# Banded attention in a decoder kernel: products of query and key in pairs of half-heads, four pairs of a chunk made by GpSimd

## The reference

```python
deltas = [0, 1, ..., 40, 128, 96, 384]      # distances to a key, J = 44
q, k, v = split(x @ w_qkv)                  # 16 heads of 16 features
idx   = arange(T)[:, None] - deltas         # T = 112 tokens
valid = idx >= 0
scores = einsum('bhtd,bhtjd->bhtj', q, k[idx] * (1 + scale_embed)) / sqrt(16)
scores = where(valid, scores + pos_bias.T, -max)
out   = einsum('bhtj,bhtjd->bhtd', softmax(scores), v[idx]) * if_gain
return out @ w_out
```

## Time and profile before

| what | value |
|---|---|
| median of 3 runs | 3439.84 us (3436.94 to 3442.88) |
| profiled execution | 3413.12 us, its span (first to last instruction) 3411.2 us |
| span's share of PE, DVE, ACT, POOL | 90%, 53%, 35%, 29% |
| banded attention | about 21 us (first product) to 325.8 us of the span |
| TensorE's granted clock in its four chunks | 1.00 of full speed |

### The profile page before, as it was taken

One profiled execution on the slowest core, in us unless ns is written; L12 is line 12 of the kernel. 1 busy time (PEld: TensorE's weight loads), 2 busy tenths in 40 slices (PEclk: granted clock), 3 DMA queues, 4 the chain that ended last, 5 costly groups with the idle time before them and its releaser, 6 DMA issues. The chain is left out here.

```text
span 3411.2 us, 72275 instructions
## 1 busy us (share of the span) xinstructions
PE 3068.7 (90%) x29076; PEld 2124.1 (62%) x29076; DVE 1814.2 (53%) x4513; ACT 1181.2 (35%) x2319; POOL 995.6 (29%) x822
## 2 busy tenths in 40 slices
PE   8997999999988888889678999699997999889989
PEld 3434555555667865658345555489997886666656
DVE  7897544453334655433776666543333763455543
ACT  1223333332233431313326665222222652244433
POOL 1001443343102111426248878321111211104001
PEclk9998999999998999989889999799998999999989
DMA  4223000000222022527211110378886200121100
GB/s 156 65 75 100 10 9 18 9 9 0 54 58 26 7 52 74 150 79 255 70 33 31 32 31 19 110 292 329 328 328 230 77 2 13 37 73 51 49 14 19
DMA packets 174741, 287.70 MB, mean 84 GB/s; under 512 B 79393, under 2 KB 145025, under 8 KB 165102
## 3 DMA queue, kind: packets, MB, share of 16 engines
q1 hardware_dynamic: 166958, 263.07, 24.0%
q0 software_dynamic: 7488, 20.46, 1.8%
HBM read 245.07 MB, written 28.48 MB: 80 GB/s over the span
## 5 line engine op out<-in xcount | busy, mean ns | idle before, releaser
L2852 PE MATMUL ps<-L_ffn_xsT,arena 128*128 128x128 f32 x2584 | 304.0, 276 | 0.7 <-DVE L_ffn_xsT L2651 0.6
L2852 PEld LDWEIGHTS ps<-L_ffn_xsT,arena 128*128 128x128 f32 x2584 | 296.3, 193 | 3.6 <-DVE L_ffn_xsT L2651 3.5
L842 POOL TENSOR_TENSOR L_xattn_rn<-L_xattn_ss,mhalf 125x16 f32<-125x16 f32 (+1 forms) x64 | 185.8, 2903 | 257.3 <-DVE L_xattn_ss L905 257.3
L3534 POOL TENSOR_TENSOR L_xattn_pT<-L_xattn_pT,L_xattn_keep 125x678 int32<-125x678 int32 x128 | 190.4, 1509 | 62.6 <-ACT L_xattn_pT L3789 62.6
L162 POOL TENSOR_TENSOR rstd<-nsc,mhalf 112x4 f32<-112x4 f32 (+2 forms) x26 | 40.2, 1545 | 556.0 <-DVE nsc L155 555.0
L2750 ACT ACTIVATE L_ffn_silu<-ps,arena 128x128 f32<-128x128 f32 x280 | 102.9, 368 | 269.2 <-PE ps L2852 254.0
L2660 DVE SCALAR_TENSOR_TENSOR L_ffn_hT<-ps,arena,L_ffn_silu 128x128 f32<-128x128 f32 x280 | 98.0, 350 | 155.3 <-ACT L_ffn_silu L2750 155.1
L2529 POOL DMA_INDIRECT L_ffn_rows_out<-L_ffn_ys,L_ffn_dest x78 | 79.6, 1021 | 319.8 <-DVE L_ffn_ys L2669 304.1
L1019 PE MATMUL ps<-arena,L_xattn_cT 128*125 128x512 f32 x384 | 166.1, 592 | 0.0
L723 PE MATMUL ps<-L_attn_prod,arena 128*32 128x448 f32 (+28 forms) x672 | 153.5, 492 | 11.5 <-DVE L_attn_prod L523 10.9
L2865 PE MATMUL ps<-arena,L_ffn_hT 128*128 128x256 f32 x646 | 153.0, 381 | 5.5 <-ACT L_ffn_ys L2759 5.4
(11 more groups left out here) (616 smaller groups left out, 6753.2 us busy)
## 6 DMA issues: line engine op xcount, KB each, us to landing
arena<-in_L_ffn_up SPq DMA_DIRECT2D x35, 2056.0 KB, 8.1
arena<-in_L_ffn_down SPq DMA_DIRECT2D x35, 1152.0 KB, 8.6
L_xattn_ctxT<-in_ctxT SPq DMA_DIRECT2D x48, 375.0 KB, 3.7
arena<-in_L_ffn_up SPq DMA_DIRECT2D x43, 384.0 KB, 4.5
L_attn_a<-L_attn_skew SPq DMA_DIRECT2D x16, 784.0 KB, 5.2
L_xattn_ctx<-in_ctx SPq DMA_DIRECT2D x30, 375.0 KB
arena<-L_xattn_kp SPq DMA_DIRECT2D x64, 93.8 KB, 3.3
L_xattn_mask<-in_mask SPq DMA_DIRECT2D x32, 164.1 KB, 8.4
```

What stands on the lines that cost most here:

```text
L842: nc.gpsimd.tensor_tensor(rn[0:r, i], ss[0:r, i], core.mhalf[0:r, 0:H], ALU.pow).then_inc(po_r.step("root", i), 1)
L2852: ins = nc.tensor.matmul(ps[:, 2 + b % 4, half * TS:(half + 1) * TS], self.up(i % WU, k, half * HM + m), xsT[:, i % 2, k], start=(k == 0), ...
L3534: nc.gpsimd.tensor_tensor(p, p, keep[:, n % 2].unsqueeze(1).to_broadcast([SP_, 2, ST * TP]), ALU.mult).then_inc(po_e.step("kept", half), 1)
```

## The change

- **Pairs.** One instruction makes the products of both halves of a distance: 42 instructions of twice the size in place of 84. `turn_of` is changed with it: in a block of 16, matmuls i and i+2 are now the two halves of one distance and go to the same column group; four matmuls in a row are groups 0, 1, 0, 1, then 2, 3, 2, 3. A pair fills slots `i % 8` and `(i + 2) % 8`; its instruction waits for both slots to be free (`before`). The ring no longer shifts by chunk: the first pair of a chunk waits for matmul 82 of the chunk before.
- **Fewer masked tokens.** Where the accumulator already holds finite numbers (everywhere but in the first two blocks of chunk 0), the even distance of a group is computed only for the tokens that its group needs. In those two blocks of chunk 0, both halves are computed for all tokens.
- **Subtraction in memory order.** `below` walks `e` as it is stored, with the maximum repeated over the distances.
- **GpSimd.** Pairs 15, 23, 31 and 39 of each chunk are made by GpSimd, which waits for the same slots and counts on a semaphore of its own (`po_i`).

The diff, cut to its core:

```diff
-        ve_x, ve_i, ve_g = one("vector", "xn", U), one("vector", "prod", NI), one("vector", "biased", NG)
+        ve_x, ve_i, ve_g = one("vector", "xn", U), one("vector", "prod", NI // 2 - SHARE), one("vector", "biased", NG)
+        po_i = one("gpsimd", "prod", SHARE)
...
             at, groups = i % 16, -(-size(i // 16) // 32)
-            c, b, odd = at % groups, at // groups % KD, at // groups // KD
+            apart = groups // 2 or 1
+            c, b, odd = at // (apart * KD) * apart % groups + at % apart, at // apart % KD, at // groups // KD
...
-            return 0 if odd == 0 and b == 0 else self.DIST[p]
+        def first_of(n):
+
+            apart = -(-size(n // 8) // 32) // 2 or 1
+            return n // 8 * 16 + n % 8 // apart * KD * apart + n % apart, apart
+
+        def start(c, i):
+
+            p, _, _, odd = turn_of(i)
+            if odd:
+                return self.DIST[p]
+            return 0 if c == 0 and i < 32 else min(self.DIST[p:p + 2])
+
+        def made(c, n):
+
+            if n % 8 == 7:
+                return (po_i, c, n // 8 - 1) if n > 8 else (ve_i, c, n)
+            return (ve_i, c, n - max(n // 8 - 1, 0))
+
+        def before(i):
+
+            return i - RING if i >= RING else max(n for n in range(NI) if n % RING == i) - NI
+
+        def products(eng, own, c, n):
+            i, apart = first_of(n)
+            if n == 0 or own is nc.gpsimd:
+                eng.wait_ge(ac_q.sem, ac_q.at(c, "qk", 2 * KD - 1))
+            used = max(before(i), before(i + apart))
+            if used >= 0:
+                eng.wait_ge(pe_i.sem, pe_i.at(c, "used", used))
+            elif c:
+                eng.wait_ge(pe_i.sem, pe_i.at(c - 1, "used", NI + used))
+            j, t0, at = self.DIST[turn_of(i)[0]], start(c, i), i % RING
+            by, _, m = made(c, n)
+            own.tensor_tensor(prod[:, at:at + apart + 1:apart, :, t0:T], q[:, c % 2].rearrange("p b (u t) -> p b u t", u=U)[:, :, :, t0:T],
+                              k[c % 2][:, :, :, PAD + t0 - j:PAD + T - j], ALU.mult).then_inc(by.step("prod", m), 1)
...
             norm_pool(core, norm)
+            products(pool, nc.gpsimd, 0, 15)
             nc.gpsimd.memset(k[1], 0.0).then_inc(ready, 1)
             nc.gpsimd.memset(v[1], 0.0).then_inc(ready, 1)
+            for c in range(NCH):
+                for n in range(15 if c else 23, NI // 2, 8):
+                    products(pool, nc.gpsimd, c, n)
...
-                nc.vector.tensor_tensor(by_head(e[c % 2][:, u]), by_head(e[c % 2][:, u]), mx[:, u, :].unsqueeze(2).to_broadcast([T, H, J]),
+                row = e[c % 2][:, u].rearrange("p (j h) -> p j h", h=H)
+                nc.vector.tensor_tensor(row, row, mx[:, u, :].unsqueeze(1).to_broadcast([T, J, H]),
...
-                    product(c, i)
+                    if i % 2 == 0:
+                        if made(c, i // 2)[0] is ve_i:
+                            products(dve, nc.vector, c, i // 2)
...
-                ten.wait_ge(ve_i.sem, ve_i.at(c, "prod", i))
+                by, _, m = made(c, pair_of(i))
+                ten.wait_ge(by.sem, by.at(c, "prod", m))
```

25 lines of the change are left out of this document (7 added, 18 removed).

## The result

The changed kernel takes 3445.56 us (median of 20 runs, 3439.83 to 3453.0) beside 3440.37 us for the kernel before (20 runs on the same chip): ratio 1.0015, 95% interval 1.0009 to 1.0021. It is 5 us slower where 10 us faster was forecast. The time is inside the range (3415 to 3450), the sign is wrong.

The account below looks back on a forecast made before the run. VectorE and TensorE were taken to run in lockstep, TensorE's pace limiting the middle chunks. Chunks +1.0, -2.6, -3.0, -5.2 and ending -0.4 made -10.2 us: 3439.8 to 3429.6, range 3415 to 3450.

Parts of the forecast that it names:

- Products, VectorE's time: VectorE's products, paired and with fewer masked tokens: -4.7 us in each of chunks 1 to 3, -2.6 in chunk 0.
- Subtraction: VectorE's subtraction in memory order, 1.21 to 0.77 us: -0.44 each, four in each of chunks 1 to 3, -1.8.
- The ending's -0.4: In the ending only the first subtraction counts, -0.4 us; the others sit behind the transfers.
- GpSimd's share: VectorE rid of 3.6 us per chunk but blocked 4.0 (chunk 0: 5.5) by GpSimd's products: net +0.4, chunk 0 +1.9.
- TensorE's own work: TensorE's matmuls in chunks 1 to 3: fewer tokens -1.7 us, runs of one column group +1.0, net -0.7 per chunk.
- What TensorE lets through: Share of VectorE's gain that shortens chunks: half of TensorE's waits in chunks 1 and 2 (-3.0, -3.4), -5.0 in chunk 3.
- New waits: First pair of a chunk waits for matmul 82: +1.2, +0.6, +0.6 us at the boundaries; shrunken lead +0.5 per chunk.
- the lead shrinks from 8 products to 5 or 6 ... taken +0.5: Pairs need two free slots, so VectorE's lead over TensorE shrinks: bounds 0 and +2 us per chunk, taken +0.5.
- the first (eaten up, 3440): Rival: TensorE bounds chunks 1 and 2 and GpSimd blocks fully, together +0.6 us; 3440, between 3434 and 3446; chance 0.25.
- The second: Rival: GpSimd is free, streaming products don't block VectorE's, -3.6 us per chunk for the share; together -27, 3413; chance 0.12.
- The third, the slower one: Rival: GpSimd can't get the port from dense VectorE products, +2.0 us at ten places; +8 in all, 3448; chance 0.18.

Follow-up runs that it names:

- sub_alone: Kernel before with only the subtraction in memory order; the two middle chunks fell by 0.93 and 1.00 us, the last by 1.4.
- no_share: Changed kernel with all 42 pairs on VectorE, none on GpSimd; 72.38 us per middle chunk, 52.6 us in chunk 0, as slow as the changed kernel.
- ring_on: Changed kernel with the ring of slots running on over the end of a chunk; the stop at a chunk's start was worth 0.8, 0.9 and 0.9 us.
- ring12_no_share: Changed kernel with twelve slots, all 42 pairs on VectorE and the context loaded by ScalarE's queue; 69.57 us per middle chunk.
- singles_masks: Kernel before with only the subtraction in memory order and the changed kernel's masks; 12 us faster than before (0.35%, interval 0.24 to 0.47%).
- ring12_share123: Changed kernel with twelve slots, GpSimd's share in chunks 1 to 3 only, context loaded one block earlier than in ring12_no_share; ratio 0.9977 to the kernel before.
- ring12: Changed kernel with twelve slots, context loaded by SyncE after the last matmul; chunks together 11.9 us shorter than the changed kernel's, ending lost 6.6.
- fills_first: Changed kernel with GpSimd's clearing of k[1] and v[1] put ahead of its first pair; chunk 0 1.1 us shorter, chunk 3 1.5 us longer.
- singles_c0_busy: singles_masks_c0 with 15 more matmuls in the ending, results read by nobody; the ending takes 40.6 us.
- singles_masks_c0: singles_masks with the masks of the kernel before in the first two blocks of chunk 0; chunk 0 fell by 1.10 us to 48.88.

## Why the prediction was wrong

From before to after there is a ladder of rungs (column "last"): subtraction, 262.73 to 259.53, -3.2 us; masks, to 253.66, -5.9; order, to 256.04, +2.4; pairs in eight slots, with the stop at the chunk's start, to 265.50, +9.5 (1.9, 2.9, 2.9 and 1.8 by chunk); share, to 264.78, -0.7. The good half of the change was worth 9 us, the other half cost 11.

- *Products, VectorE's time.* Right: pairs of 840 to 872 elements take 1.03 to 1.07 us as records (by the formula 0.94 to 0.98, and the overlap), and VectorE's busy time in chunk 1 fell by 8.4.
- *Subtraction.* Right: 0.86 us, and half let through. The ending's -0.4 did not come (sub_alone: +0.1).
- *GpSimd's share.* The step put +0.4 us on VectorE per chunk and +1.9 in chunk 0. That a product waits for GpSimd's is right, but it was counted too often. In chunk 1 no_share's 59.93 us less 3.6 would be 56.3 and 57.23 was measured, so 0.9 was blocked, not 4.0; one VectorE product is stretched there, at 142.06, from 1.09 to 1.75 us. In chunk 0 four are, by 3.0 us in all, not 5.5. The net in time is -1.14 in the middle chunks and +1.35 in chunk 0: the sizes were off by 0.5 to 1.5 us and the sign in the middle. In chunk 0 most of the cost came by a way not named: the fills beside L198.
- *TensorE's own work.* -0.7 as a net was mis-sized: the masks gave 2.25, 2.22, 2.02 us (with VectorE's shorter products in it) and the order took 0.56, 0.55, 0.60, -1.4 to -1.7 in all. The reading of the order was loose, too: in the four runs named a group comes back after one other (3, 2, 3, 0), not directly. Chunk 0, for which I had counted the wider first blocks on VectorE alone, lost 0.6 by the masks and 0.7 by the order.
- *What TensorE lets through.* Half of VectorE's gain, -5.0 in chunk 3: true of the subtraction (0.93, 1.00 and 1.4 of 1.8), untrue of the pairs. Pairs took 3 us per chunk off VectorE and gave, even in twelve slots, +0.1 in the middle chunks and -0.3 in chunk 3 (66.05 against 66.35). This step failed as well, in chunk 3 above all. It stood on a sum of waits and not on what each edit does to the moment at which a product is there.
- *New waits.* **This is the step that failed most.** At the chunk's start 1.2, 0.6, 0.6 were forecast, 0.8, 0.9, 0.9 measured (ring_on): right in sum. But "the lead shrinks from 8 products to 5 or 6 ... taken +0.5" was 2 us per chunk: no_share less ring12_no_share, 2.8, less the 0.85 of the start; in chunk 0, 4.55 less 0.8. Its upper bound of 2 was the truth in chunks 1 to 3, and chunk 0 went beyond it. The reason for the low value, that the full lead had been used up in only 14 places for 12.4 us, is a reading of a queue with eight units of one, and says nothing of one with four units of two. The place to look at was the dense run of matmuls that ends with matmul 75: the loss turned up right behind it.

The forecast by chunk was +1.0, -2.6, -3.0, -5.2 and -0.4 for the ending; measured +4.65, -0.88, -0.89, -0.83 and +1.0. Of the 13.3 us between the sums, the lead explains some 7.8: 3.75 us of chunk 0 and 2 of each other chunk, less the 0.5 counted. In chunk 3 another 2.9 are missing, which the pairs did not let through. The ending's 1.4 are not explained by any edit here: it varies from 40.1 to 42.6 us among the kernels that load the context as before does.

Of the rivals, the first (eaten up, 3440) has the nearest time but not the reason: GpSimd didn't block fully, and the middle chunks came down to 68.9 us (singles_masks), so TensorE did not bound them at 72. The second fell (products beside GpSimd's take 1.5 to 2.2 us, so streams do block). The third, the slower one, forecast 3448 by GpSimd not getting in. Its mechanism exists, in three places of sixteen: VectorE products that started behind GpSimd's pair ran ahead of it, once each at 110.8 and 182.0 us, and three of them here (GpSimd, then VectorE):

```profile
235.96 3.85 POOL L409 TENSOR_TENSOR L_attn_prod<-arena 128x696 f32<-128x696 f32 x1 [21.80 <-PE ps L756]
```

```profile
235.38 0.86 DVE L526 TENSOR_TENSOR arena<-arena,L_attn_mx 112x672 f32<-112x672 f32 x1
236.16 2.36 DVE L409 TENSOR_TENSOR L_attn_prod<-arena 128x648 f32<-128x648 f32 x3
238.44 1.32 DVE L532 TENSOR_REDUCE L_attn_den<-arena 112x16 f32<-112x672 f32 x1
```

GpSimd's pair, 1.51 us beside a reduction (at 99.19), started during the subtraction and was done only 1.4 us after the reduction began; three products that started after it went through first. But as no_share is as slow as after, the rival's account of the loss is wrong.

Left open: the changed kernel's 5.2 us are 1.9 more than the stage of its profiled execution shows. A half-clock stretch in chunk 3 (three of the four kernels with after's schedule there had one at this place) and a longer ending would be enough, but no profile of such an execution of after exists. Why chunk 3 takes 66.4 us in ring12_share123 and 65.2 in ring12 wasn't followed (0.8 of it arises between matmuls 24 and 28, and ring12 is the one with a half-clock stretch ahead of them), nor why pairs with the old masks and twelve slots stay 0.8 us above single products (72.32 against 71.20 and 0.3 for the order) where with the new masks they are level.

## What to carry over

Count a ring of buffers in the producer's units: eight slots filled two at a time are a lead of four at most, and of fewer where the two of a pair come free at different moments, and an engine that got faster by pairing will wait for it. The price falls due where the consumer takes unit after unit without other work. Split a bundle of edits and take each to the engine that bounds: here shorter matmuls and a faster subtraction were worth 10 to 12 us by themselves (stage, whole), and the larger part, fewer and longer VectorE instructions, was worth nothing with twelve slots and cost 9.5 with eight. Where two engines run in lockstep, one that is busy for 65.6 of 72.5 us may still give its saved time back as waiting.

## What the runs showed of the hardware

- A stop of 1.93 us of TensorE, with work up to it and behind it, went with some 3 us at 1.2 GHz in three kernels and not in a fourth with the same stop (after); those three took 1.5 us more. What a half-clock stretch costs depends on where it falls: the one at matmul 20 of chunk 3 (no_share, fills_first) was made up by matmul 24. In chunk 0 singles_c0_busy had the clock at 0.5 from 22.0 to 25.4 us and took 48.89 us, singles_masks_c0, with the same code there and the clock at 1.00, 48.88: where products set the pace, the half clock cost nothing. The Trainium skill (TensorE: Matmul & The Clock Gate, What's actually happening) says that idleness throttles the array and that activity releases it. The three kernels agree, and the fourth, whose clock stayed at 1.00 there, shows that the same stop does not always do it.
- GpSimd's memory fills, which read nothing, held VectorE's tensor-scalar instructions (one input in SBUF): 3.27 us for four in place of 1.37. The Trainium skill (SBUF — State Buffer, Who interferes with whom) counts tensor_scalar among the instructions that can take the port pair that VectorE and GpSimd share; the rows agree.
- The same section says that whoever issues first gets the port pair. In the place above (235.96 us) three VectorE products that started 0.2 to 1.7 us after GpSimd's pair of products ran ahead of it, as far as the recorded starts tell: VectorE, working without a gap, kept the port until a reduction came. Where VectorE's own instruction had an input in PSUM (L515, L546), GpSimd's pair got in and held up the VectorE product behind it (36.08, 249.62 us). Here the measurement decides against the page.
- Two transfers of the context, started by ScalarE 4.5 us ahead of a small dependent write, went with a way from that write to its read of 4.75 us (ring12_no_share) in place of 2.4 (after, and ring12, where the load comes later).
